# Two orders changed in one turn of an attention: SyncE's stores ahead of its loads, and VectorE's distances behind the maxima

## What is computed

```python
# first attention, causal, 16 heads of 32 channels; q from x, k and v are ctx itself
scores = jnp.einsum('bhqd,bhkd->bhqk', q, kj) * SCALE      # masked above the diagonal
out = softmax(scores) @ v
x = x + tanh(g_xattn[0]) * attention(layernorm(x), ctx, ctx)
# weights of the first feed-forward net, ternary by groups of 64
scale = jnp.clip(jnp.mean(jnp.abs(w_g), axis=-1, keepdims=True), 1e-08, None)
w_hat = jnp.clip(jnp.round(w_g / scale), -1, 1) * scale
# second attention: k = rms_norm(ctx @ k_img_w + b), v = ctx @ v_img_w + b
```

## Time and profile before

| | before |
|---|---|
| median of 3 runs | 1069.67 us (1069.55 to 1070.2) |
| profiled execution, as a run | 1072.09 us |
| its span in the profile | 1070.3 us |
| TensorE busy | 1046.8 us, 98% |
| VectorE busy | 832.5 us, 78% |
| ScalarE busy | 585.6 us, 55% |
| GpSimd busy | 119.2 us, 11% |

### The profile page before, as it was taken

One profiled execution on the slowest core, in us unless ns is written; L12 is line 12 of the kernel. 1 busy time (PEld: TensorE's weight loads), 2 busy tenths in 40 slices (PEclk: granted clock), 3 DMA queues, 4 the chain that ended last, 5 costly groups with the idle time before them and its releaser, 6 DMA issues.

```text
span 1070.3 us, 24338 instructions
## 1 busy us (share of the span) xinstructions
PE 1046.8 (98%) x9770; PEld 617.9 (58%) x9770; DVE 832.5 (78%) x1440; ACT 585.6 (55%) x893; POOL 119.2 (11%) x212
## 2 busy tenths in 40 slices
PE   8899999999999999999999999999999999999998
PEld 3555555555777777777777664444444444444444
DVE  4978888878777675675766577898888888888987
ACT  4766677767433332333333347638585857583633
POOL 1101001010000000000000211321111111110110
PEclk9999999999999999999999999999999999999999
DMA  9575654642331230321302022215343434341223
GB/s 361 170 235 192 197 155 147 205 132 68 131 89 33 57 80 1 80 60 40 80 23 57 20 88 62 60 43 96 80 89 80 80 87 88 78 70 46 41 59 80
DMA packets 121199, 102.77 MB, mean 96 GB/s; under 512 B 94720, under 2 KB 95232, under 8 KB 120832
## 3 DMA queue, kind: packets, MB, share of 16 engines
q1 hardware_dynamic: 121088, 101.21, 34.6%
HBM read 65.54 MB, written 12.58 MB: 73 GB/s over the span
## 4 chain that ended last, share of the span: by engine, by line
PE 82%; DVE 7%; DMA 4%; issue 3%; ACT 3%; SPq 1%; ACTq 0%; DVEq 0%
PE bank L704 10%; PE bank L705 10%; PE bank L792 10%; PE bank L810 9%; PE bank L669 8%; PE bank L918 7%; PE bank L936 4%; PE bank L906 4%; PE bank L869 3%; PE bank L891 2%; PE bank L606 2%; PE bank L549 2%; PE bank L622 2%; PE bank L634 2%; PE bank L574 2%
## 5 line engine op out<-in xcount | busy, mean ns | idle before, releaser
L704 PE MATMUL bank<-ARENA,W 128*128 128x256 f16 x1024 | 227.3, 273 | 0.7 <-issue 0.7
L705 PE MATMUL bank<-ARENA,W 128*128 128x256 f16 x1024 | 227.3, 273 | 0.0
L1112 ACT ACTIVATE ARENA<-ARENA 128x512 f16<-128x512 f32 (+1 forms) x96 | 66.8, 707 | 144.7 <-DVE ARENA L1760 132.0
L792 PE MATMUL bank<-W,ARENA 128*128 128x512 bf16 x512 | 120.8, 379 | 0.6 <-DVE ARENA L1766 0.6
L918 PE MATMUL bank<-W,ARENA 128*128 128x512 bf16 x512 | 117.8, 379 | 1.8 <-DVE W L1921 0.5
L810 PE MATMUL bank<-ARENA 128*128 128x512 f32 x256 | 118.4, 603 | 0.2 <-DVE ARENA L1847 0.2
L669 PE MATMUL bank<-ARENA 128*128 128x512 f32 x256 | 118.0, 603 | 0.6 <-DMA ARENA<-in_wkv 0.5
L704 PEld LDWEIGHTS bank<-ARENA,W 128*128 128x128 bf16 x1024 | 100.2, 98 | 19.1 <-issue 1.1
L705 PEld LDWEIGHTS bank<-ARENA,W 128*128 128x128 bf16 x1024 | 100.2, 98 | 18.0
L2225 POOL TENSOR_TENSOR ARENA<-ARENA 128x2 f32<-128x2 f32 (+1 forms) x72 | 51.7, 718 | 490.2 <-DVE ARENA L1534 258.3
L1760 DVE SCALAR_TENSOR_TENSOR ARENA<-bank,ARENA 128x512 f32<-128x512 f32 x64 | 48.0, 750 | 65.7 <-PE bank L705 62.3
(11 more groups left out here) (190 smaller groups left out, 1742.7 us busy)
## 6 DMA issues: line engine op xcount, KB each, us to landing
W<-in_w SPq DMA_DIRECT2D x48, 512.0 KB, 4.2
ARENA<-in_w SPq DMA_DIRECT2D x24, 512.0 KB, 3.6
kv_store<-ARENA SPq DMA_DIRECT2D x32, 256.0 KB, 4.4
W<-kv_store SPq DMA_DIRECT2D x15, 512.0 KB, 4.5
ARENA<-in_ctxT SPq DMA_DIRECT2D x8, 512.0 KB, 3.8
X<-in_x SPq DMA_DIRECT2D x8, 512.0 KB, 6.8
ARENA<-in_ctx SPq DMA_DIRECT2D x8, 512.0 KB, 6.1
out<-X SPq DMA_DIRECT2D x15, 256.0 KB, 2.3
```

Of the source, the lines that this page charges most:

```text
L704: pe.matmul(bank[:, i * S:(i + 1) * S], W0[:, at:at + P], xt_half(b, 0)[:, k, :], start=(k == 0), stop=False)
L705: mm = pe.matmul(bank[:, i * S:(i + 1) * S], W0[:, at:at + P], xt_half(b, 1)[:, k, :], start=False, stop=(k == KD - 1))
L792: mm = pe.matmul(banks[6 + t], hx(q, what)[:, i * S + t * P:i * S + (t + 1) * P], W0[:, UP_AT + m * D:UP_AT + (m + 1) * D], start=(m == 0 ...
L1112: return act.activation(to, src, ACT.Copy)
```

## The change

SyncE, turn 1 only: store (0, 2) is issued ahead of w0 load 5 and x 2, and stores (1, 0) and (1, 1) right behind store (0, 3), ahead of w1 loads 3 and 4 and w0 load 7. VectorE, turn 1 only: distances (0, 1) are made behind the rows of the second maxima, right before ternary (0, 1), and no longer between the maxima of the third and the fourth scores. No instruction is added or taken away.

```diff
@@ SyncE
             for turn in range(1, NB + 1):
                 f, b = turn, turn - 1
+                if turn == 1:
+                    store_kv(b, 2)
                 load_w0(3 * turn + 2)
                 load_x(turn + 1)
-                store_kv(b, 2)
+                if turn > 1:
+                    store_kv(b, 2)
                 load_values(turn)
                 load_w1(3 * turn - 1)
                 load_w0(3 * turn + 3)
                 store_kv(b, 3)
+                if turn == 1:
+                    store_kv(f, 0)
+                    store_kv(f, 1)
                 load_w1(3 * turn)
                 load_w1(3 * turn + 1)
                 load_w0(3 * turn + 4)
-                if f < NB:
+                if 1 < f < NB:
                     store_kv(f, 0)
                     store_kv(f, 1)
@@ VectorE
                     if turn == 1:
                         a_scores(b, 2)
-                    a_distance(b, 1)
                     if turn > 1:
+                        a_distance(b, 1)
                         a_ternary(b, 1)
                         a_scores(b, 2)
@@
                     a_max_rows(b, 1)
                     if turn == 1:
+                        a_distance(b, 1)
                         a_ternary(b, 1)
                     a_distance(b, 2)
```

## The result

The change makes the kernel slower: 1072.63 us median of 17 runs (1072.00 to 1074.14) against 1069.84 of 17 runs of the kernel before (1069.37 to 1072.54), a ratio of 1.0024 with a 95% interval of 1.0017 to 1.0031. That is 2.8 us, outside the range of the prediction on its upper side. The profiled execution of after took 1073.66 us, its span is 1071.9.

A forecast was written before the change was run, and what follows sets the result against it. TensorE, busy 1046.8 of 1070.3 us, was taken as the bound. +0.41 for VectorE's lateness and -1.5 for the clock made -1.1: span 1069.2, median 1068.6 from 1069.67, range 1066.8 to 1071.2.

The forecast's parts named there:

- The clock gives it back: TensorE, 64 to 68 us: with its idle time in shorter gaps the clock stays up, -1.5 us.
- +0.41: TensorE's probabilities (1, 0) start at 64.33 instead of 63.92, behind VectorE's copy of the maxima: +0.41 us.
- my own 2.06 us: VectorE reaches turn 2's first maxima at 53.33 instead of 51.27, 2.06 us late.
- part 2: VectorE, turn 1: moving distances (0, 1) brings TensorE hardly any gain; turn 2's first maxima come 2.06 us late.
- Part 1: Store (0, 2): ScalarE's copy 1.0 to 1.1 us sooner, but GpSimd's add delays VectorE's product by 1.0; third maxima 0.65 later.
- Rival A: GpSimd's add and VectorE's product don't meet in turn 1; third maxima gain 0.35, sum -2.0, 1067.7; chance 0.20.
- Part 3: Stores (1, 0), (1, 1): ScalarE's 5.80 us wait at 60.04 goes; load 3 lands about 54.3; copy (1, 2) 4.6 earlier.
- Rival D: The stores change nothing, since load 3 behind store (1, 1) takes over the wait; 0 us, 1069.7; chance 0.03.
- Rival C: TensorE waits 1.9 us before turn 1's fourth scores and the clock falls there; 1070.1 to 1071.6; chance 0.18.

The follow-up runs named there:

- the unchanged kernel's second profile: The kernel before, run and profiled again with nothing edited: 1069.91 us median, ratio 1.0000; profiled execution 1069.37, span 1067.6.
- The stores with both adds waiting: Kernel before with all three stores early and GpSimd's adds to (1, 0) and (1, 1) waiting for VectorE's products (0, 0) and (0, 2): 1068.43 us, again 1068.40.
- the waits alone: Kernel before with GpSimd's adds to (1, 0) and (1, 1) waiting for VectorE's products, stores and distances as before: 1069.37 us, ratio 0.9994.
- The first add's wait: Whole change, with GpSimd's add to (1, 0) also waiting for VectorE's product of ternary (0, 0): 1071.47 us, ratio 1.0017 to the kernel before.
- the late stores: Kernel before with only stores (1, 0) and (1, 1) early, store (0, 2) and distances where they were: 1069.66 us, ratio 0.9998.

## Why the prediction was wrong

**The step that failed is "The clock gives it back", the term of -1.5 us in the sum.** The fall of the clock at 64 us was real in the execution that was read and is absent from the unchanged kernel's second profile. Where it isn't, there is nothing to give back. The prediction subtracted the term from a span of 1070.3 and carried the difference to a median of 1069.67, though that execution, 1072.09 as a run, lay 2.4 us above the median. It had that number before it and called the rest "untouched"; it should have asked where those 2.4 us were. The second profile's span is 2.7 us shorter, and 2.3 us of that arise in the very stretch it priced, between the projections (1, 3) and (2, 0): 1.0 since store (1, 0) landed later, the rest by the clock. With 0 for this term the same sum is +0.4 and not -1.1. And the +0.41 was counted from the late probabilities at 63.92; from the second profile's (62.67, or 62.9 with that execution's later start) it is 1.4.

**A wait was missed behind the probabilities (1, 0).** The prediction followed VectorE to the copy of the maxima and stopped there, 0.41 us late. The projection (2, 0) needs the bank that the reciprocals read, two VectorE steps later. In the execution that was read, they start at 63.82, covered by the slow clock (the projection at 66.79). Had I added my own 2.06 us to 63.82, they were at 65.88 and the projection 0.51 later at 66.39, against 65.88 by the probabilities (64.33 and 1.55 for what lies between, 62.67 to 64.22 in the unchanged kernel's second profile). So 0.5 us more. Against an execution at full clock the account is simpler: VectorE has 0.12 us of slack there, so that 2.06 us late cost 1.9, and the same working would have given 1069.7 + 1.9 = 1071.6. With the 0.5 us that part 2 was short by (below) it is 1072.1, and the executions without a fall have 1072.17; the 6 falls in the 17 runs lift the median to 1072.63.

**Part 1** was right in every step: ScalarE's copy at 32.53 with no store wait, GpSimd's add at 33.30 over line 1614, 1.65 us where I had put 1.0 us more than 0.69 (the product ends 0.54 behind the add), third maxima at 36.33 for 36.06, where this execution is 0.29 later from its start (line 1614 at 33.51, its twin at 33.22 in the earlier trace rows). Rival A fell. By the rule of the Trainium skill (GPSIMD Engine Reference, Specifications) the early store costs VectorE a meeting, and the trace agrees: 1.64 or 1.65 us in the four profiles with store (0, 2) early and an add that doesn't wait, 0.69 for the same product in all five in which the add was put behind it and the store was early too.

**Part 2** had the place and was 0.5 us small. In the execution without a fall, the fourth scores are at 38.28 (forecast 38.25), the turn of x at 40.69 (40.65). The copy of the maxima is at 42.56 and not at 42.13: the turn of the maxima follows the turn of x with no gap, and the copy starts 0.79 behind it, where it was 0.38 behind a turn that stood after a gap of 0.83. That is 0.41. From the copy to the first maxima it took 11.35 us and not 11.20. The meeting with line 1604 saved 0.14 over the one with 1608, as forecast, but the prediction moved the distances with the 2.38 us that they take in front of a reduction (37.15 to 39.53); in front of the product of the ternary they take 2.50 (42.77 to 45.27). Together 53.33 becomes 53.91. From there on the 10.65 us to the next copy (53.91 to 64.55) and the 0.35 to the probabilities hold to 0.01. The whole move against the unchanged kernel, with 0.29 taken off for a later start (GpSimd's inverse root, line 2225 before and 2232 after, at 30.54 and 30.83): first maxima 51.04 to 53.91, 2.58 us; the projection (2, 0) 64.22 to 66.96, 2.45. The end of the span follows it: 1067.6 to 1070.5, 2.9 with the 0.29.

**Part 3** was right that no copy of ScalarE waits for a store, and had load 3 landing 54.3 where it was 55.18 (57.04 in the execution with the fall); the copy (1, 2) came at 56.24 and the cover held. Rival D's condition, the load taking over the wait as the bound, is refuted by the stores alone: TensorE waits for VectorE. But the part was worth nothing with VectorE as late as it was. The stores with both adds waiting, and the waits alone, show it from both sides: 1068.4 and 1069.4.

**Rival C** came true at its place and by its mechanism in the profiled execution, and by their clock and their time in eight more of the 23 runs: the gap was put at 1.9 us and measured 1.91 and 1.92, and the fall cost 1.6 (1.5 was put down). Its time was too low for the same two reasons as the forecast's. The first add's wait shortens the gap (0.96), and no clock below 1.000 is on record in 22 runs of the two versions with this wait and the change's distances, nor in the 44 of the others with the wait, nor in the 11 of the distances alone (0.46): that supports the gap as the cause. The price is another matter. The stores alone had the gap and 7 falls in 11 runs and lost nothing by them, and in the late stores' profile an avoided meeting made up for a fall. In the changed kernel the fall moves VectorE's copy of the maxima (42.56 to 44.24), with all distances behind it. Why the stores alone don't pay is not shown. Why the clock fell behind it in 9 runs and stayed in 14 is open: nothing that I changed tells them apart.

Of the final loss, then, by the table: the two waits alone bring 0.4 (1069.8 to 1069.4), the distances' place costs 1.8 us (1070.2 against 1068.4), the meetings of GpSimd with VectorE and the falls of the clock behind the longer gap some 2.4 to 2.7 (1072.6 or 1072.9 against 1070.2), and against this the stores bring 1.0 (1069.4 to 1068.4), which can be had only when the meetings are gone; in the kernel before as it is they bring nothing (1070.0 beside 1069.8).

## What to carry to other kernels

Compare the profiled execution with the median of the runs before pricing anything in it; if it stands above by more than the gain sought, find the stretch that holds the excess, and count nothing there as winnable. When a wait is removed, go on past the next instruction to each later one that needs the engine which is now last, and write down its slack: here two engines stood 0.1 us apart and neither edit alone could win. Before a transfer is moved, look at what its earlier landing will start on GpSimd, and over which VectorE product; two waits in GpSimd's program took 2.4 us off the changed kernel.

## What the runs showed of the hardware

- A GpSimd add of 1.27 us and a two-operand VectorE product of 0.69 us do not share their time: met, the product takes 1.64 to 1.79 and ends 0.54 to 0.56 behind the add, most of its own 0.69. The add waits too when VectorE is already in a product: 1.70 us at 49.56 in the late stores alone, and 1.59 at 50.23 in the kernel after, with the next product, line 1604, ending 0.55 behind it. The Trainium skill (SBUF — State Buffer, Terms) calls the shared port pair exclusive and held for the full instruction; the rows agree but for some 0.14 us, by which the part of the product behind the add is shorter than 0.69.
- A copy of 0.29 us from PSUM started 0.38 us behind the start of a turn that stood after a gap, and 0.79 behind one that directly followed eight other matmuls. Matmul ends are modelled in these records, so that some of the 0.41 may be the record's; VectorE's start is not.
- TensorE's granted clock fell behind one idle stretch of 1.91 us in one execution and stayed at 2.4 GHz behind the same stretch in others (1.91 with the stores alone and with the first store alone, 1.92 in the changed kernel again); it fell behind 1.90 us with the late stores alone. The changed kernel has two groups of times by it, 1.6 us apart; the stores alone, with 7 falls in 11 runs, have one.
